# Masked graph attention on one core: tiles 8 to 31 take their means and squared deviations from ScalarE, tiles 0 to 7 share one chain

## The reference

```
h      = relu((x - mean(x)) / sqrt(var(x) + 1e-5))       # per row of 128
H      = h @ W_fc + b_fc
score  = (H @ a[:128])[:, None] + (H @ a[128:])[None, :] + b_att
alpha  = softmax(where(A > 0, score, -1e9), axis=1)
out    = x + alpha @ H
```

## Time and profile before

| | |
|---|---|
| median of 3 runs | 187.31 us (187.17 to 188.09) |
| the profiled execution | 186.87 us, its span 185.1 |
| TensorE, VectorE, ScalarE, GpSimd busy | 159.5, 132.6, 63.7, 9.5 us |
| transfers over the span | 71.64 MB |

### The profile page before, as it was taken

One profiled execution on the slowest core, in us unless ns is written; L12 is line 12 of the kernel. 1 busy time (PEld: TensorE's weight loads), 2 busy tenths in 40 slices (PEclk: granted clock), 3 DMA queues, 4 the chain that ended last, 5 costly groups with the idle time before them and its releaser, 6 DMA issues.

```text
span 185.1 us, 2660 instructions
## 1 busy us (share of the span) xinstructions
PE 159.5 (86%) x866; PEld 114.6 (62%) x866; DVE 132.6 (72%) x424; ACT 63.7 (34%) x136; POOL 9.5 (5%) x33
## 2 busy tenths in 40 slices
PE   0509689999955799999999999999999999999970
PEld 0307456675632686867768676686876866877740
DVE  0599999989796996978665487696773625459941
ACT  2353170703604963222232422442242424021020
POOL 2103201300003020000000000000000000000000
PEclk9999969999999799999999999999999999999996
DMA  5999999999999999999999999999999999997112
GB/s 171 384 441 427 425 428 432 430 421 436 420 428 418 439 425 425 436 421 426 420 423 428 428 425 423 425 425 425 426 422 425 438 422 421 418 395 272 70 60 58
DMA packets 8370, 71.64 MB, mean 387 GB/s; under 512 B 929, under 2 KB 1698, under 8 KB 3490
## 3 DMA queue, kind: packets, MB, share of 16 engines
q1 hardware_dynamic: 7776, 71.18, 91.9%
q10 hardware_dynamic: 578, 0.26, 0.6%
HBM read 69.34 MB, written 2.10 MB: 386 GB/s over the span
## 4 chain that ended last, share of the span: by engine, by line
PE 51%; DVE 21%; DMA 21%; ACT 2%; issue 2%; SPq 0%; DVEq 0%
PE bank L807 21%; PE bank L813 19%; DMA ring<-adj 17%; PE bank L831 6%; DVE mask L463 5%; DVE low L486 4%; DMA x_sb<-x 4%; PE bank L855 3%; DVE mask L472 3%; ACT weighted L359 2%; PE bank L845 1%; DVE stats L480 1%; DVE x_sb L594 1%; DVE low L574 1%; DVE x_sb L601 1%
## 5 line engine op out<-in xcount | busy, mean ns | idle before, releaser
L807 PE MATMUL bank<-mask,high 128*128 128x512 f32 x256 | 79.4, 412 | 14.3 <-DVE mask L472 6.9
L463 DVE TENSOR_SCALAR mask<-ring 128x1024 fp32r<-128x1024 int32 (+2 forms) x66 | 59.6, 920 | 29.5 <-DMA ring<-adj 18.2
L813 PE MATMUL bank<-mask,low 128*128 128x512 f32 x256 | 76.4, 401 | 0.0
L807 PEld LDWEIGHTS bank<-mask,high 128*128 128x128 f32 x256 | 47.2, 193 | 33.8 <-issue 8.7
L813 PEld LDWEIGHTS bank<-mask,low 128*128 128x128 f32 x256 | 49.7, 194 | 11.0
L405 ACT ACTIVATE mask<-ring,half_steep 128x512 fp32r<-128x512 int32 x43 | 28.8, 718 | 58.7 <-DMA ring<-adj 38.8
L831 PE MATMUL bank<-mask,w_cols 128*32 128x512 bf16 x256 | 20.3, 402 | 0.0
L371 ACT ACTIVATE relu<-x_sb,neg_mean 128x128 f32<-128x128 f32 x32 | 9.8, 390 | 13.3 <-DVE neg_mean L495 13.3
L831 PEld LDWEIGHTS bank<-mask,w_cols 128*32 128x32 bf16 x256 | 5.9, 96 | 11.4 <-issue 7.2
L480 DVE BATCH_NORM_STATS2 stats<-x_sb 128x6 f32<-128x128 f32 x32 | 7.2, 280 | 6.7 <-DMA x_sb<-x 6.7
L359 ACT ACTIVATE weighted<-relu,w_over_std 128x128 f32<-128x128 f32 x32 | 10.1, 391 | 3.3 <-DVE w_over_std L563 3.2
(11 more groups left out here) (80 smaller groups left out, 61.7 us busy)
## 6 DMA issues: line engine op xcount, KB each, us to landing
ring<-adj SPq DMA_DIRECT2D x18, 2048.0 KB, 16.2
ring<-adj SPq DMA_DIRECT2D x16, 1536.0 KB, 12.5
ring<-adj SPq DMA_DIRECT2D x3, 1024.0 KB, 9.1
out<-x_sb SPq DMA_DIRECT2D x7, 256.0 KB, 13.4
x_sb<-x SPq DMA_DIRECT2D x1, 1024.0 KB, 20.3
ring<-adj SPq DMA_DIRECT2D x4, 256.0 KB, 16.7
x_sb<-x SPq DMA_DIRECT2D x2, 256.0 KB, 5.4
x_sb<-x SPq DMA_DIRECT2D x1, 512.0 KB, 9.8
```

The costliest lines, as they stand in the source:

```text
L463: nc.vector.tensor_scalar(mask[:, n % MASKS, 0:cols], ring[:, n // 2 % RING, begin:begin + cols], 0.0, None, ALU.is_gt).then_inc(masks_rea ...
L807: nc.tensor.matmul(bank[:, b, :], high[:, t, :], mask[:, n % MASKS, cols], start=(t == 0), stop=False)
L813: last = nc.tensor.matmul(bank[:, b, :], low[:, t, :], mask[:, n % MASKS, cols], start=False, stop=(t == T - 1))
```

## The change

Four things change. SP issues x of tiles 0 to 3 and of 4 to 7 ahead of both halves of the first pair. Tiles 0 to 7 take their means and 1/std in one chain (`SPANS`). For tiles 8 to 31 VectorE computes no bn_stats: ScalarE takes the negative mean of a tile as the accumulated sum of a Copy with scale -1/128 (`late_means`), and the sum of squares of x minus mean as that of a Square (`late_squares`), each with its result thrown into the still unused `low` and `high` of that tile. VectorE's chain for them starts from this sum. And the orders of both engines are written anew.

```diff
+SPANS = [(0, 8), (8, 16), (16, 32)]
...
-            for i in range(2):
-                load_x(i)
+            load_x(0)
+            load_x(1)
...
+            def late_means(t0, t1):
+                if t0 in (SPANS[1][0], SPANS[2][0]):
+                    act.wait_ge(x_landed[STAGE_OF[t0]], 16)
+                for t in range(t0, t1):
+                    nc.scalar.activation(low[:, t, :], x_sb[:, t, :], ACT.Copy, scale=-1.0 / D,
+                                         accum_out=neg_mean[:, t:t + 1]).then_inc(late_means_ready, 1)
+
+            def late_squares(t0, t1):
+                for t in range(t0, t1):
+                    act.wait_ge(late_means_ready, t - LATE + 1)
+                    nc.scalar.activation(high[:, t, :], x_sb[:, t, :], ACT.Square, bias=neg_mean[:, t:t + 1],
+                                         accum_out=var[:, t:t + 1]).then_inc(squares_ready, 1)
...
-                nc.vector.tensor_tensor(mean_diff[:, tiles], stats[:, tiles, 4], stats[:, tiles, 1], ALU.subtract)
...
+                else:
+                    dve.wait_ge(squares_ready, tiles.stop - SPANS[1][0])
+                    step(nc.vector.tensor_scalar(var[:, tiles], var[:, tiles], 1.0 / D, EPS, ALU.mult, ALU.add), 0)
...
             def between_2(i):
-                if i < 8:
-                    dot_of(8 + i)
+                if i < 4:
+                    dot_of(16 + i)
+                elif i < 8:
+                    mask_quarter(12, i - 4)
+                else:
+                    dot_of(12 + i)
...
-            for n in range(10, 13):
-                for t in range(*[(16, 22), (22, 28), (28, 32)][n - 10]):
-                    last = stats_of(t)
...
+            for n in range(8, 12):
                 mask_unit(n)
-            deviations(3, between_3)
...
+            deviations(2, between_2)
+            for t in range(24, 32):
+                last = dot_of(t)
+            scores(3, last)
+            mask_unit(13)
             row_weights(3)
+            mask_unit(14)
+            split(6)
+            mask_unit(15)
+            split(7)
```

More of the change, by code:

```diff
@@ L190, in gnn_kernel @@
         means_ready = sem("means_ready")
+        late_means_ready = sem("late_means_ready")
+        squares_ready = sem("squares_ready")
         relu_ready = sem("relu_ready")
@@ L374, in _, with row_weights_of @@
+            def row_weights_of(k):
+                tiles = slice(*STAGES[k])
+                act.wait_ge(d_ready, k + 1)
+                nc.scalar.activation(w_j[:, tiles], d_raw[:, tiles], ACT.Exp, bias=minus_bound[:]).then_inc(w_ready, 1)
+            act.wait_ge(means_ready, 1)
+            relu_tiles(0, 4)
             act.wait_ge(v_in_psum, 1)
             nc.scalar.copy(v_rows[:].rearrange("p c d -> p (c d)"), ps_v).then_inc(v_rows_ready, 1)
[L376 to L391, removed]
@@ new lines, in _ @@
+            relu_tiles(4, 8)
+            row_weights_of(0)
+            act.wait_ge(w_over_std_ready, 1)
+            weigh(0)
+            weigh(1)
+            take_high(0)
+            weigh(2)
+            take_high(1)
+            late_means(8, 12)
+            take_high(2)
+            late_means(12, 16)
+            row_weights_of(1)
+            late_squares(8, 12)
+            act.wait_ge(w_over_std_ready, 2)
+            weigh(3)
+            late_squares(12, 16)
+            take_high(3)
@@ new lines, in _ @@
+            relu_tiles(8, 16)
+            act.wait_ge(lines_in_psum, 1)
+            nc.scalar.copy(lines[:], ps_lines).then_inc(lines_ready, 1)
+            late_means(16, 24)
+            row_weights_of(2)
+            late_means(24, 27)
+            act.wait_ge(w_over_std_ready, 3)
+            weigh(4)
+            weigh(5)
+            take_high(4)
+            take_high(5)
+            late_means(27, 32)
+            late_squares(16, 32)
+            relu_tiles(16, 32)
+            row_weights_of(3)
@@ L393, in copy_den @@
+            act.wait_ge(w_over_std_ready, 4)
+            for u in range(6, 10):
+                weigh(u)
+                if u > 6:
+                    take_high(u - 1)
+            take_high(9)
             def copy_den(g):
@@ L627, in _ @@
             scores(1, last)
-            for t in range(11, 16):
-                last = stats_of(t)
-            link(last)
-            link(sum_of_halves(2))
-            negative_mean(2).then_inc(means_ready, 1)
+            mask_unit(2)
             row_weights(1)
@@ L637, in _ @@
             mask_unit(5)
-            deviations(2, between_2)
+            deviations(1, between_1)
             scores(2)
```

96 lines of the change are left out of this document (36 added, 60 removed).

## The result

The changed kernel takes **186.01 us** (median of five runs, 185.87 to 186.24), before 187.31: ratio 0.992, 95% interval 0.990 to 0.994. I had forecast 187.3 and no change. The profiled execution took 186.24, its span 184.3 (before 186.87 and 185.1).

What follows compares the result with a forecast made beforehand. Saturated adjacency transfers and TensorE were taken to meet at 156.2, with TensorE's work fixing the rest. TensorE's lead of some 4 us ended waiting at the landing, summing to 0: forecast 187.3, range 186.3 to 189.9.

Steps and rivals of the forecast that it cites:

- The bytes are the same, so the landings are: Adjacency loads never stop, so no earlier mask speeds them; the last group's first pair still lands at 154.94.
- the transfers lose less: Rival, transfers from 119.55 to 154.94: shifted instruction fetches take up to 1.0 us off, 186.3; chance 0.13.
- Transfers and TensorE arrive together: At the last group's first units: both arrive at 156.2, so an earlier TensorE only meets the landing at 154.94.
- Its lead on TensorE, which I priced at zero: After tile 16: TensorE some 4 us ahead, keeps about 1.4, waits with it at 154.94; 0 at the end.
- The sum against the profiled 186.87, moved to 187.31: Whole kernel: no change against the profiled 186.87; the median of three runs, 187.31, gave the forecast 187.3.
- The end: From the landing at 154.94 on: time fixed by TensorE's work, 22.03 us busy, then last results; left alone by the change.
- x and the single chain: Kernel's front: d_raw of tiles 0 to 3 at 10.5, of 4 to 7 at 15.5; VectorE waits for x only once.
- Tile 16: TensorE starts this tile at about 59 instead of 61.3, without the idle 3.07; idles about 2 near 50 to 52.
- none at 156: Clock rival: TensorE's wait at the landing of 154.94 lowers its clock, costing 1.7, 189.0; chance 0.04.
- The margin of 63: Added operations stay hidden under transfers until tile 16 starts after about 63, at a = 0.29; then 0.48 us per 0.01.
- The accumulator's price: ScalarE's 48 means and squares: each pays a for handing out its accumulator, taken as 0.2, between nothing and 0.39.
- the first rival: ScalarE becomes the bound from a = 0.29: 189.2 at a = 0.33, 192.1 at 0.39; chance 0.21.

Runs made afterwards that it cites:

- three kernels (187.46, 187.44, 187.50): Before without 28 VectorE running sums: 187.46; before without 64 VectorE instructions behind unit 23: 187.44; before with the last group's first pair in two transfers: 187.50.
- landing and TensorE's lateness together: Before without 28 running sums on VectorE and without 16 TensorE matmuls of the low parts of tiles 17 to 20: 186.26, ratio 0.994.
- before again: The kernel before, unchanged, run once more: 187.34, ratio 1.000; its profiled execution took 187.29.
- the two starts measured: Changed kernel with three extra ScalarE squares over eight tiles: tile 16 at 62.13, time 185.67; with six: tile 16 at 64.09, time 187.13.
- x first: Before with only both first pieces of x asked for ahead of the first adjacency halves: 187.24, ratio 1.000.

## Why the prediction was wrong

**The bytes are the same, so the landings are: this step failed.** The prediction named 154.94 as fixed and found a sum of 0. The landing came at 154.50 after, against 154.94 and 155.28 in two profiles of before. The shortening of VectorE's program moves an 8 KB instruction packet from 149, just ahead of the landing, to 180, behind all loads, and a packet in that place costs the landing 0.96 to 0.98. Put back by 90 memsets it brings a landing of 155.95, taken from before by 28 instructions one of 154.14, with 45 memsets (no packet there) one of 154.58. The landing is 0.4 to 0.8 earlier rather than 0.97, since the changed kernel was 0.2 to 0.5 later up to the last step. That a packet holds up one of the 16 engines is inferred: one landing signal of 16 trails, but the trace doesn't say which engine carried the packet. Why a packet of 0.32 us costs up to 1.0 stays open. The rival "the transfers lose less" had this mechanism, its sign and 186.3, with 0.13. I gave it little as I couldn't place the fetches, though the packets of rows 12 could have been placed window by window. The us that it missed between 119.55 and 154.94 is this slip: 5.87 for 4.90 in the last step.

**Transfers and TensorE arrive together.** Right, and more than I made of it. The landing taken away alone left the median where it was in three kernels (187.46, 187.44, 187.50), though in the second the spans are 0.35 shorter; landing and TensorE's lateness together gave 1.2 us (187.42 to 186.26 beside each other). The lateness alone stays without a clean run, so how the gain divides between the two isn't shown. The change removes both. Its lead on TensorE, which I priced at zero since it meets the landing, lets the earlier landing count in full, as the rival had it.

**The sum against the profiled 186.87, moved to 187.31.** I took the profiled execution for typical; of the two profiles of before it had the earlier landing. Against it the span is 0.77 shorter. Against before again, the 1.19 us of span divide into 0.83 up to is_empty (178.64 to 177.81) and 0.36 behind it, of which I had counted neither.

**The end.** Held fixed too, and it failed with the landing: this is the part that takes the time below the rival's 186.3, an attribution by the profiles and not by a run of its own. Before, a packet follows VectorE's closing branch at 182.4, among the last stores; after, an 8 KB packet comes earlier, at 180.0, and none lies between 181 and 182.5.

**The parts that held.** x and the single chain: d_raw at 10.25 and 15.21 for 10.5 and 15.5, one wait for x, at 4.32. Tile 16 at 58.79 for 59, the idle of 2.13 at 50.58 and one spell at the low clock there, none at 62 and none at 156. TensorE waited 0.79 at 155.78 for my 1 to 1.6: 0.73 and 0.70 of its lead had gone to waits for masks at 80.88 and 90.67. The margin of 63 lies between the two starts measured. My equation gives a = 0.296 for it; I wrote 0.29.

**The accumulator's price** was mis-sized: means start every 0.29 and squares every 0.386, so a, the part over my 0.21 and 0.305, is about 0.08, not 0.2; reading takes 0.19, half of it under its neighbours. So the first rival was never near, and the CAST of tile 16 ended at 53.6, not at 55 to 58. TensorE came to it at 58.79 all the same, busy until then. By the figures of the Trainium skill (ScalarE: Activation LUTs, What ACT_TABLE_LOAD costs) the prediction's estimate was 0.09; the trace, with 0.08, agrees.

## What to carry over

When two arrivals meet within a few tenths, removing one can show nothing: take both away in one run before calling either harmless. Where transfers are saturated, the code is traffic as well: look where the instruction queues' packets fall before and after, and don't take a landing for fixed because the bytes are. Look at a second profile of before when its median and its profiled time differ (here by 0.44) by more than what you forecast.

## Unexpected on the hardware

- Near VectorE's 67th, 200th, 325th and 448th record stood packets of 8 KB and about 0.32 us, and the landing moved by over 1 us with one packet more (154.50 to 155.95) or one fewer (155.28 to 154.14). The Trainium skill (Runtime: NRT & Kernel Launch, Instruction fetch mechanics) speaks of 16 KiB blocks and calls the cost of crossing into the next one mostly hidden. The trace has packets of both sizes, 16 KB on q8 and 8 KB on q14, and here the cost wasn't hidden from the transfers.
- VectorE's closing branch took 0.24 us to its next record in the changed kernel and 0.62 in before, where a packet follows; the last store landed 4.95 behind is_empty in the one and 5.6 in the other.
- Of before's 22 runs above 188.1, 21 had a granted clock below 0.98, as had 97 of all 133, so a low clock alone doesn't make a late run. Behind one and the same idle time of 3.06 or 3.07 ahead of tile 16, TensorE's clock stayed up in one profile (before again), was low for 3.4 us in another (the first) and for 6.8 in a third (x first). That the lead of some 4 us covers this scatter is likely and not shown.
